# One run over sixteen groups of heads: the next batch prepared one ahead, its parts read back group by group, the splits on GpSimd

## The chip, the core and the metric

The kernel runs on one core of a Trainium2 chip. A core has five engines with an instruction queue each: TensorE (PE, with its weight loads as PEld), VectorE (DVE), ScalarE (ACT), GpSimd (POOL) and SyncE (SP), which here only issues DMAs. All work out of an on-chip memory (SBUF); matmuls write to a second one (PSUM, eight banks of 128 x 512 float32). Engines wait for each other on semaphores. The metric is the device time of one execution in microseconds (us), lower is better.

## What is computed

Four stages run one after the other on x of shape (4, 1024, 128), each between layernorms: a local attention, a mixture of experts, a global causal attention and a six-layer local transformer. The change is in the third, `fourier_attention_stage`. Cut to what matters:

```python
b, t, d = x.shape                                   # 4, 1024, 128; 16 heads of 8
q, k, v = jnp.split(x @ Wqkv.T, 3, axis=-1)         # then heads(...)
logits = jnp.einsum('bhqd,bhkd->bhqk', q, k) * scale
logits = logits + _fourier_bias(alpha, beta, t)[None]   # sum of cos and sin of i - j, per head
logits = jnp.where(causal[None, None], logits, -jnp.inf)
attn = jax.nn.softmax(logits, axis=-1)
out = jnp.einsum('bhqk,bhkd->bhqd', attn, v)
return out.transpose(0, 2, 1, 3).reshape(b, t, d) @ Wout.T
```

## The kernel before

**Parts.** Scores are made by bf16 matmuls whose rows are three-way splits of float32 values: a high part, and two remainders. ACT makes the high part (`parts[:, 0, :]`), and `split` makes the other two, a subtraction and a cast each. A head's rows in `qp` and `kp` (98 partitions x 16 heads x 1024 tokens) are 48 rows of q and k parts, 48 rows of the bias's cosine basis, and two rows for the negated row maximum. As q and k come with features on the partitions, the parts go out to DRAM (`q_dram`, `k_dram`) and come back rearranged, 8 partitions at a time: `d h t` in the code. The k side of the basis (the f parts) takes the same way once, at the start.

**A batch** has a preparation (PE turns x, multiplies by the q, k and v weights; ACT copies out; the splits on DVE; write and read-back by SP), four groups of four heads, and a finish (normalised output turned, times w_out, copied to y_all by DVE).

**A group** has two passes. The maxima pass: PE makes 48 tiles of scores (L737) into two banks, DVE reduces each to its row maxima (L866), then the negated maxima are turned by PE (L781), split in two bf16 rows by DVE (`c_mrow`, L891 to L895) and written over DRAM into `qp` (L687, L689). The second pass: PE makes 40 tiles of transposed scores (L752), ACT takes the exponent (L834), PE multiplies by v (L766). `groups()` overlaps them: the maxima pass of group g + 1 is interleaved with the second pass of group g. In front of a batch stands a maxima pass alone, `body(None, ...)`, and at its end a second pass alone, `body(NG - 1, ..., False)`. PE enters the batch's first maxima pass only when all parts of the batch are placed. Lines here are those of the kernel before.

The order of work on each engine is the order of the code; `Fori` is a loop on the engine itself, and `bass.ds(g, ...)` an address from its register. Every engine runs the same loops, and all of SP's DMAs share one queue.

Of the kernel before, what the change touches and what calls it, by code (L numbers as in the profile page):

```python
# [568 lines left out]
def fourier_attention_stage(nc, y_all, const, dram):  # L569
# [12 lines left out]
    with ExitStack() as ctx:  # L582
# [21 lines left out]
        ve = sb("ve", [P, TB, H, DH + 1])  # L604
# [12 lines left out]
        q_dram = nc.dram_tensor("c_q_scratch", (3, P, SEQ), BF16, kind="Internal").ap()  # L617
        m_dram = nc.dram_tensor("c_m_scratch", (2, GROUP * TB, P), BF16, kind="Internal").ap()
        k_dram = nc.dram_tensor("c_k_scratch", (3, P, SEQ), BF16, kind="Internal").ap()
# [16 lines left out]

        c_in, zeroed, f_done, f_ready, parts_ready, out_dram_done, placed = (
# [11 lines left out]
        def groups(eng, b, body):  # L649

            NG = H // GROUP
            body(None, b * NG - 1, True)
            with eng.Fori(0, NG - 1) as g:
                body(g, b * NG + g, True)
            body(NG - 1, b * NG + NG - 1, False)

        with nc.Block() as block:
            @block.sync
            def _(eng):
                for dst, src in ((ident_b, "ident_b"), (mask_q, "c_mask_q"), (mask_k, "c_mask_k"), (w_qkv, "c_w_qkv"),  # L660
                                 (w_out, "c_w_out"), (place, "c_place"), (basis, "c_basis")):
                    eng.dma_start(dst[:], dram[src]).then_inc(c_in, 16)
# [6 lines left out]
                eng.dma_start(k_dram.rearrange("r p t -> p r t"), kparts[:]).then_inc(out_dram_done, 16)  # L669
                eng.wait_ge(out_dram_done, 16)  # L670
                for r in range(PARTS):
                    eng.dma_start(kp[ROWS + 8 * r:ROWS + 8 * r + 8, :, :],
                                  k_dram[K_PART[r]].rearrange("(h d) t -> d h t", d=DH)).then_inc(placed, 16)
                eng.wait_ge(placed, 16 * PARTS)
                with eng.Fori(0, BATCH) as b:
# [3 lines left out]
                    eng.dma_start(k_dram.rearrange("r p t -> p r t"), kparts[:]).then_inc(out_dram_done, 16)  # L679
# [1163 lines left out]
```

## Time and profile before

| | |
|---|---|
| median of three runs | 6686.75 us (6683.01 to 6694.7) |
| the profiled execution | 6685.4 us, its span 6683.6 us |
| busy in the span | PE 79%, DVE 63%, ACT 44%, POOL 39% |
| the changed stage | 1294.36 to 2956.30 us of the span |
| granted PE clock, mean | 0.895 of full speed |

The span is what the profiler records between the first and last instruction. The stage in question is a quarter of it. The shares of the whole span say little about it; GpSimd, for one, does nothing in it but two memsets.

### The profile page before, as it was taken

The numbers are of one execution on the slowest core, as the hardware profiler recorded it, in microseconds if no ns is written. First come the engines' busy times: TensorE is split into PE (matmuls) and PEld (weight loads), VectorE is DVE, ScalarE is ACT, GpSimd is POOL, SyncE is SP. The second block draws the span as 40 slices with busy tenths as digits, with TensorE's granted clock in tenths as the row PEclk, the third lists the DMA queues.
The fourth block names the chain that finished last, engine by engine and source line by source line (L and its number), as shares of the span: only waits on it lengthen the run. The fifth ranks groups of instructions, "written<-read, shape, count | busy, mean of one in ns | idle before, by whom it ended". The sixth has DMA issues, their size and how long they took to land. (4 is left out here: it accounts for less than half of the span.)

```text
span 6683.6 us, 148998 instructions
## 1 busy us (share of the span) xinstructions
PE 5256.6 (79%) x55030; PEld 3176.6 (48%) x55030; DVE 4233.4 (63%) x5698; ACT 2953.9 (44%) x4797; POOL 2630.1 (39%) x1392
## 2 busy tenths in 40 slices
PE   4735777348488584867999999999999999999996
PEld 3623444212122121214666666666666666666664
DVE  4353111324142332348999989898889888989995
ACT  0001222113123131325666666666666666666663
POOL 0000000000000000017777777677766766777773
PEclk8657889769788686889999999999999999999997
DMA  0000100130200102002111211211121112111111
GB/s 18 0 8 14 28 28 28 20 43 0 29 0 1 28 1 28 1 15 64 36 38 37 57 36 36 57 35 37 34 57 36 35 41 53 36 36 42 35 38 46
DMA packets 153483, 202.80 MB, mean 30 GB/s; under 512 B 40920, under 2 KB 79714, under 8 KB 151662
## 3 DMA queue, kind: packets, MB, share of 16 engines
q1 hardware_dynamic: 153360, 201.17, 13.2%
q8 instruction: 76, 1.25, 0.1%
q14 instruction: 47, 0.39, 0.0%
HBM read 63.67 MB, written 11.53 MB: 11 GB/s over the span
## 5 line engine op out<-in xcount | busy, mean ns | idle before, releaser
L99 POOL TENSOR_TENSOR ln_post_rstd<-ln_post_var,neg_half 128x8 f32<-128x8 f32 x16 | 26.8, 1672 | 2919.6 <-DVE ln_post_var L80 2919.6
L1704 POOL TENSOR_TENSOR d_rnorm<-d_sq_clip,neg_half 128x32 f32<-128x32 f32 x192 | 1048.4, 5461 | 62.6 <-DVE d_sq_clip L1536 61.9
L1694 POOL TENSOR_TENSOR d_qk_swap<-d_qk_raw,d_rot 128x512 f32<-128x512 f32 x768 | 961.0, 1284 | 17.9 <-ACT d_qk_raw L1379 14.0
L866 DVE TENSOR_REDUCE c_mx<-c_ps 128x1 f32<-128x512 f32 (+3 forms) x768 | 416.6, 556 | 775.7 <-PE c_ps L737 771.9
L834 ACT ACTIVATE c_pt<-c_ps 128x512 f32<-128x512 f32 (+1 forms) x640 | 354.3, 554 | 1117.6 <-PE c_ps L752 1115.7
L1153 PE MATMUL d_pair<-d_wqkv,d_xin 128*128 (+1 forms) x1536 | 753.4, 614 | 93.5 <-DVE d_probs L1557 40.6
L766 PE MATMUL c_ps<-c_pt,c_vg 128*32 128x512 f32 (+3 forms) x1536 | 628.3, 506 | 4.7 <-DVE c_ots L871 4.7
L1681 POOL TENSOR_TENSOR d_probs<-d_probs,d_prec 128x1024 f32<-128x1024 f32 x192 | 369.2, 1923 | 454.3 <-DVE d_prec L1568 454.3
L1165 PE MATMUL d_pair<-ident,d_qk_part 128*128 128x128 f32 x3072 | 424.4, 277 | 140.3 <-DVE d_qk_part L1547 137.7
L1165 PEld LDWEIGHTS d_pair<-ident,d_qk_part 128*128 128x128 f32 x3072 | 353.2, 141 | 321.1 <-issue 241.9
L1518 DVE TENSOR_TENSOR d_qk_part<-d_qk_raw,d_rot 128x1024 f32<-128x1024 f32 x384 | 471.4, 1228 | 48.9 <-issue 38.3
L1379 ACT ACTIVATE d_qk_raw<-d_pair 128x512 f32<-128x512 f32 x768 | 424.4, 591 | 94.3 <-PE d_pair L1153 90.3
L1547 DVE TENSOR_TENSOR d_qk_part<-d_qk_part,d_rnorm 128x2048 f32<-128x2048 f32 x192 | 442.2, 2303 | 27.8 <-POOL d_rnorm L1704 4.6
L1543 DVE TENSOR_TENSOR d_qk_part<-d_qk_part,d_qk_swap 128x2048 f32<-128x2048 f32 x192 | 440.0, 2292 | 30.7 <-issue 27.6
L1153 PEld LDWEIGHTS d_pair<-d_wqkv,d_xin 128*128 128x128 f32 x1536 | 280.9, 193 | 349.9 <-issue 332.1
L1532 DVE TENSOR_REDUCE d_sq_sum<-d_qk_sq 128x32 f32<-128x2048 f32 x192 | 433.6, 2258 | 9.7 <-ACT d_qk_sq L1386 6.6
L1173 PE MATMUL d_pair<-d_wqkv,d_xin 128*128 (+1 forms) x768 | 414.4, 621 | 11.3 <-ACT d_kt L1396 9.3
L1402 ACT ACTIVATE d_ot<-d_pair 128x1024 f32<-128x1024 f32 x192 | 196.5, 1023 | 470.7 <-PE d_pair L1209 470.7
L1386 ACT ACTIVATE d_qk_sq<-d_qk_raw 128x1024 f32<-128x1024 f32 x384 | 395.5, 1058 | 6.1
L1205 PE MATMUL d_pair<-d_band,d_v 128*64 128x128 f32 x6144 | 379.8, 276 | 9.3 <-issue 2.0
L1205 PEld LDWEIGHTS d_pair<-d_band,d_v 128*64 128x64 f32 x6144 | 333.5, 137 | 97.2 <-issue 97.0
L557 DVE TENSOR_TENSOR b_part<-b_py,b_b 128x512 f32<-128x512 f32 x64 | 44.2, 691 | 526.1 <-PE b_py L452 526.1
(248 smaller groups left out, 9676.4 us busy)
## 6 DMA issues: line engine op xcount, KB each, us to landing
d_band<-d_own_t SPq DMA_DIRECT2D x768, 64.0 KB, 2.0
d_band<-d_prev_t SPq DMA_DIRECT2D x576, 64.0 KB, 2.0
d_v_prev<-d_v SPq DMA_DIRECT2D x192, 128.0 KB, 2.3
b_w<-in_L_ffn_w SPq DMA_DIRECT2D x64, 256.0 KB, 3.3
d_band_prev<-d_prev_t SPq DMA_DIRECT2D x192, 64.0 KB, 2.0
d_wqkv<-in_L_ffn_Wqkv SPq DMA_DIRECT2D x6, 1536.0 KB, 8.8
c_kp<-c_k_scratch SPq DMA_DIRECT2D x30, 256.0 KB
c_qp<-c_q_scratch SPq DMA_DIRECT2D x24, 256.0 KB
```

The costliest lines, as they stand in the source:

```text
L766: mm = eng.matmul(ps[32 * hh:32 * hh + 32, OB, q0:q0 + nq], vg[:, kt, hh, :], pt[j % 4][:, col:col + nq], start=(opens and k == 0), stop=T ...
L866: eng.tensor_reduce(mx[:, hh, qt, k0 // 512:k0 // 512 + 1], ps[:, S1B[c % 2], 0:nk], AX.X, ALU.max).then_inc(mx_done, 1)
L1153: eng.matmul(bank(QK_AT[u][c]), xin[p][:, :], wqkv[:, bass.ds(par, 1), c * 512:(c + 1) * 512].rearrange("p l n -> p (l n)"), start=True, s ...
L1165: mm = eng.transpose(bank(TURN_AT[u][c])[:, j * P:(j + 1) * P], qk_part[1 - p][:, which, h:h + 2, :].rearrange("p h d -> p (h d)"), ident[ ...
L1205: eng.matmul(op[r:r + 64, h // 2, :].rearrange("p (w t) -> p w t", t=WIN), v_sb[1 - p][:, h * DH:(h + 1) * DH], band[1 - p][:, :, at, :], ...
L1379: eng.activation(qk_raw[:, c // 2, 8 * (c % 2):8 * (c % 2) + 8, :].rearrange("p h d -> p (h d)"), bank(QK_AT[u][c]), ACT.Copy).then_inc(qk ...
L1518: return eng.tensor_tensor(qk_part[p][:, which], qk_raw[:, which], rot[:, bass.ds(par, 1), which, 0, bass.ds(i, 1), :].rearrange("p l t d ...
L1532: eng.tensor_reduce(sq_sum[:], qk_sq[:].rearrange("p a h d -> p (a h) d"), AX.X, ALU.add)
L1543: eng.tensor_tensor(flat, flat, qk_swap[:].rearrange("p a h d -> p (a h d)"), ALU.add)
L1547: eng.tensor_tensor(heads, heads, rnorm[:, :].unsqueeze(2).broadcast_to((P, 2 * HEADS, DH)), ALU.mult).then_inc(rope_ready, 1)
L1694: mm = eng.tensor_tensor(qk_swap[:, which, :, out:out + hd], qk_raw[:, which, :, src:src + hd], rot[:, bass.ds(par, 1), which, 1, bass.ds( ...
L1704: eng.tensor_tensor(rnorm[:, :], sq_clip[:, :], neg_half[:, 0:2 * HEADS], ALU.pow).then_inc(rn_ready, 1)
```

## The change

The four batches become one run. `batches()` takes the place of `groups()`: batch 0 is prepared and the one maxima pass by itself is made; then, for three batches, the next batch is prepared, four groups run, each with the maxima pass of the group behind it (the last one with that of the next batch's first group), and the batch is finished; the last batch's four groups and finish follow. SP reads the next batch's parts back for one group at a time, into the place of the group whose second pass has just ended. v gets two buffers (`ve`), the DRAM copies one place for each batch. The splits go from DVE to GpSimd. The first three constants get a semaphore of their own.

```diff
-        ve = sb("ve", [P, TB, H, DH + 1])
+        ve = sb("ve", [P, 2, TB, H, DH + 1])
...
-        def groups(eng, b, body):
-            NG = H // GROUP
-            body(None, b * NG - 1, True)
+        PLACED = 16 * 2 * PARTS
+        def batches(eng, prepare, body, finish):
+            prepare(0)
+            body(None, 0, -1, True)
+            with eng.Fori(0, BATCH - 1) as b:
+                prepare(b + 1)
+                with eng.Fori(0, NG) as g:
+                    body(g, b, b * NG + g, True)
+                finish(b)
             with eng.Fori(0, NG - 1) as g:
-                body(g, b * NG + g, True)
-            body(NG - 1, b * NG + NG - 1, False)
+                body(g, BATCH - 1, (BATCH - 1) * NG + g, True)
+            body(NG - 1, BATCH - 1, BATCH * NG - 1, False)
+            finish(BATCH - 1)
...
-                for dst, src in ((ident_b, "ident_b"), (mask_q, "c_mask_q"), (mask_k, "c_mask_k"), (w_qkv, "c_w_qkv"),
-                                 (w_out, "c_w_out"), (place, "c_place"), (basis, "c_basis")):
+                for dst, src in ((place, "c_place"), (basis, "c_basis"), (w_qkv, "c_w_qkv")):
+                    eng.dma_start(dst[:], dram[src]).then_inc(first_in, 16)
+                for dst, src in ((ident_b, "ident_b"), (mask_q, "c_mask_q"), (mask_k, "c_mask_k"), (w_out, "c_w_out")):
                     eng.dma_start(dst[:], dram[src]).then_inc(c_in, 16)
...
+                def keep_parts(b):
                     eng.wait_ge(parts_ready, b + 2)
-                    eng.wait_ge(out_done, b)
-                    eng.dma_start(q_dram.rearrange("r p t -> p r t"), qparts[:]).then_inc(out_dram_done, 16)
-                    eng.dma_start(k_dram.rearrange("r p t -> p r t"), kparts[:]).then_inc(out_dram_done, 16)
-                    eng.wait_ge(out_dram_done, b * 32 + 48)
+                    eng.dma_start(one(q_dram, b).rearrange("r p t -> p r t"), qparts[:]).then_inc(out_dram_done, 16)
+                    eng.dma_start(one(k_dram, b).rearrange("r p t -> p r t"), kparts[:]).then_inc(out_dram_done, 16)
+
+                def place_parts(b, g):
+                    eng.wait_ge(placed, (b * NG + g) * PLACED + 16 * PARTS)
                     for r in range(PARTS):
-                        eng.dma_start(qp[8 * r:8 * r + 8, :, :], q_dram[Q_PART[r]].rearrange("(h d) t -> d h t", d=DH)).then_inc(placed, 16)
-                        eng.dma_start(kp[8 * r:8 * r + 8, :, :], k_dram[K_PART[r]].rearrange("(h d) t -> d h t", d=DH)).then_inc(placed, 16)
+                        for to, src, part in ((qp, q_dram, Q_PART[r]), (kp, k_dram, K_PART[r])):
+                            rows = src[bass.ds(b, 1), part, :, :].rearrange("l p t -> (l p) t").rearrange("(h d) t -> d h t", d=DH)
+                            eng.dma_start(to[8 * r:8 * r + 8, bass.ds(g * GROUP, GROUP), :],
+                                          rows[:, bass.ds(g * GROUP, GROUP), :]).then_inc(placed, 16)
+
+                def place_maxima(g, G):
+                    eng.wait_ge(m_ready, G + 1)
+                    ...
+                keep_parts(0)
+                eng.wait_ge(out_dram_done, 48)
+                for g in range(NG // 2):
+                    place_parts(0, g)
+                place_maxima(0, 0)
+                for g in range(NG // 2, NG):
+                    place_parts(0, g)
+                with eng.Fori(0, BATCH - 1) as b:
+                    keep_parts(b + 1)
+                    with eng.Fori(1, NG) as g:
+                        place_maxima(g, b * NG + g)
+                        eng.wait_ge(out_dram_done, b * 32 + 80)
+                        eng.sem_inc(passed, 1)
+                        eng.wait_ge(s2_ready, (b * NG + g) * N2)
+                        eng.sem_inc(passed, 1)
+                        place_parts(b + 1, g - 1)
+                    place_maxima(0, b * NG + NG)
+                    eng.wait_ge(s2_ready, (b * NG + NG) * N2)
+                    eng.sem_inc(passed, 1)
+                    place_parts(b + 1, NG - 1)
+                with eng.Fori(1, NG) as g:
+                    place_maxima(g, (BATCH - 1) * NG + g)
...
             @block.gpsimd
+                def prepare(b):
+                    split(qparts, qf, 2 * b + 2)
+                    split(kparts, kf, 2 * b + 3)
+                    eng.sem_inc(parts_ready, 1)
...
             @block.tensor
-                eng.wait_ge(c_in, 16 * CONSTS)
+                eng.wait_ge(first_in, 48)
...
-                    eng.wait_ge(placed, (b + 1) * (16 * 2 * PARTS) + 16 * PARTS)
+                    if isinstance(b, int):
+                        eng.wait_ge(c_in, 16 * CONSTS)
+                def body(g, b, G, maxima):
+                    live = g is not None
+                    if maxima:
+                        eng.wait_ge(placed, (G + 2) * PLACED + 16 * PARTS)
...
-                                head = (0 if g is None else (g + 1) * GROUP) + hh
+                            head = (0 if g is None else ((g + 1) % NG) * GROUP) + hh
...
             @block.vector
+                def prepare(b):
+                    rows = y_all[:, bass.ds(b * TB, TB), :]
+                    if not isinstance(b, int):
+                        eng.wait_ge(turned, b)
+                    eng.tensor_copy(xin[:], rows).then_inc(xin_ready, 1)
```

The bodies of a group are otherwise the same on all engines, and the diff's other lines only indent them.

PE at the start of a group run, before (the rows behind the first two products; `c_xin` is the batch's x, `ISA` a wait or register load):

```order
L707 UNCONDITIONAL_BRANCH
L707 ISA
L710 MATMUL c_ps<-ident,c_xin 128x128 x8
L715 MATMUL c_ps<-c_xt,c_w_qkv 128x512 x4
L718 MATMUL c_ps<-c_w_qkv,c_xt 128x128 x8
L721 ISA
L723 ISA
L736 MATMUL c_ps<-c_mask_q,c_ident_b 128x128
```

PE in the changed kernel, from the end of the maxima pass that stands alone (the last row of scores and the turn of `c_negm`) to the first tiles of the loop of groups:

```order
L810 MATMUL c_ps<-c_kp,c_qp 128x512
L854 MATMUL c_ps<-ident,c_negm 32x128
L659 UNCONDITIONAL_BRANCH
L659 ISA
L777 MATMUL c_ps<-ident,c_xin 128x128 x8
L782 MATMUL c_ps<-c_xt,c_w_qkv 128x512 x4
L785 ISA
L787 MATMUL c_ps<-c_w_qkv,c_xt 128x128 x8
L790 ISA
L661 UNCONDITIONAL_BRANCH
```

The preparation now stands behind a maxima pass, and what follows it is the loop of groups.

PE in the changed kernel, from the end of the loop of groups to the end of the outer loop:

```order
L854 MATMUL c_ps<-ident,c_negm 32x128
L661 REGISTER_ALU
L661 COMPARE_AND_BRANCH
L857 REGISTER_ALU
L859 MATMUL c_ps<-ident,c_on 128x128 x8
L863 MATMUL c_ps<-c_w_out,c_ont 128x128 x8
L659 REGISTER_ALU
L659 COMPARE_AND_BRANCH
```

Finish (L859, L863) now comes behind a group that carries the next batch's maxima (the turn of `c_negm`).

DVE before, at the head of its loop over batches (the splits of q and k behind the copy of x):

```order
L853 UNCONDITIONAL_BRANCH
L853 ISA
L855 COPY c_xin<-y_all 128x1024
L844 ISA
L846 TENSOR_TENSOR c_qf<-c_qf,c_qparts 128x1024
L848 CAST c_qparts<-c_qf 128x1024
```

DVE in the changed kernel at the same place, the head of its outer loop:

```order
L659 UNCONDITIONAL_BRANCH
L659 ISA
L923 ISA
L923 COPY c_xin<-y_all 128x1024
L661 UNCONDITIONAL_BRANCH
L661 ISA
L931 TENSOR_REDUCE c_mx<-c_ps 128x1
```

Behind the copy of x DVE goes straight to the first row maxima; the subtractions and casts stand on POOL now.

SP in the changed kernel, in the loop over a batch's groups (the maxima's two DMAs, then the first of the twelve of `place_parts`):

```order
L723 ISA
L708 DMA c_m_scratch<-c_mrow 32x2x128
L709 REGISTER_ALU
L710 ISA
L710 DMA c_qp<-c_m_scratch 2x4096
L725 ISA
L727 REGISTER_ALU
L699 ISA
L703 ISA
L703 REGISTER_ALU
L703 DMA c_qp<-c_q_scratch 8x4x1024
```

The read-back of a quarter (8x4x1024 where it was 8x16x1024) now stands behind each group's maxima.

## Rows read from the trace of the kernel before

**Rows 1.** The page's first line.
```profile
span 6683.6 us, 148998 instructions
```

**Rows 2.** Timeline, SP's DMA issues: start us, us, engine, line, what, count.
```profile
1294.36 0.34 SPq L662 DMA_DIRECT2D c_ident_b<-in_ident_b  x1
...
1336.49 0.41 SPq L669 DMA_DIRECT2D c_k_scratch<-c_kparts  x1
1340.10 2.73 SPq L672 DMA_DIRECT2D c_kp<-c_k_scratch  x6
1368.92 0.39 SPq L678 DMA_DIRECT2D c_q_scratch<-c_qparts  x1
...
1374.57 0.31 SPq L682 DMA_DIRECT2D c_qp<-c_q_scratch  x1
...
1379.12 4.55 SPq L682 DMA_DIRECT2D c_qp<-c_q_scratch  x1
```

**Rows 3.** Stretches: from:to, length, busy by engine (x instructions), PEclk, DMA share, GB/s.
```profile
1766.00:1834.00 68.00, 0.55 (x4) 0.35 (x4) 4.32 (x6) 0.47 (x1) 0.00 (x0) 0.52 0.50 70
...
2013.00:2087.00 74.00, 65.94 (x265) 20.32 (x265) 29.94 (x59) 22.64 (x41) 0.00 (x0) 0.89 0.00 0
...
1374.60:1432.50 57.90, 0.00 (x0) 0.00 (x0) 0.00 (x0) 0.00 (x0) 0.00 (x0) 0.50 0.52 54
```

**Rows 4.** Waits of 1294 to 2957 us: total us, times, longest us.
```profile
PE c_ps L736 <- DMA c_kp<-c_k_scratch: 291.3, 4, 84.3
```

**Rows 5.** Timeline, PE's first products and the first maxima pass [idle before <- releaser].
```profile
1326.36 3.78 PE L704 MATMUL c_ps<-c_basis,c_place 12*128 12x512 f32 x4 [81.11 <-DMA c_kp<-in_c_ones]
...
1432.51 0.29 PE L736 MATMUL c_ps<-c_mask_q,c_ident_b 128*128 128x128 bf16 x1 [84.28 <-DMA c_kp<-c_k_scratch]
```

**Rows 6.** Timeline, DVE's last c_mrow copy of a maxima pass.
```profile
1466.08 0.21 DVE L895 CAST c_mrow<-c_mrest 32x128 bf16<-32x128 f32 x1
...
1685.86 0.21 DVE L895 CAST c_mrow<-c_mrest 32x128 bf16<-32x128 f32 x1
...
1867.03 0.21 DVE L895 CAST c_mrow<-c_mrest 32x128 bf16<-32x128 f32 x1
...
2088.53 0.21 DVE L895 CAST c_mrow<-c_mrest 32x128 bf16<-32x128 f32 x1
...
2891.90 0.21 DVE L895 CAST c_mrow<-c_mrest 32x128 bf16<-32x128 f32 x1
```

**Rows 7.** Timeline, ends of groups and batches, and one preparation.
```profile
2087.30 0.39 PE L781 MATMUL c_ps<-ident,c_negm 128*32 128x128 f32 x1 [1.41 <-DVE c_negm L886]
...
2092.14 0.29 PE L750 MATMUL c_ps<-c_mask_k,c_ident_b 128*128 128x128 bf16 x1 [4.45 <-DMA c_qp<-c_m_scratch]
...
2145.69 0.26 DVE L876 RECIPROCAL c_rec<-c_ps 128x16 f32<-128x16 f32 x1 [0.84 <-PE c_ps L775]
...
2150.69 1.23 DVE L899 TENSOR_SCALAR y_all<-c_ps 128x1024 f32 x1 [4.38 <-PE c_ps L790]
2155.12 0.69 DVE L855 COPY c_xin<-y_all 128x1024 f32 x1 [3.20 <-issue]
...
2167.33 1.06 ACT L819 ACTIVATE c_ve<-c_ps 128x512 f32<-128x512 f32 x2
...
2545.39 0.26 DVE L876 RECIPROCAL c_rec<-c_ps 128x16 f32<-128x16 f32 x1 [0.84 <-PE c_ps L775]
...
2552.69 1.23 DVE L899 TENSOR_SCALAR y_all<-c_ps 128x1024 f32 x1 [6.68 <-PE c_ps L790]
...
2955.07 1.23 DVE L899 TENSOR_SCALAR y_all<-c_ps 128x1024 f32 x1 [4.38 <-PE c_ps L790]
```

**Rows 8.** Lines and sources: durations ns (mean; or min/median/max) of DVE and POOL operations.
```profile
L846 DVE TENSOR_TENSOR c_kf<-c_kf,c_kparts 128x1024 f32<-128x1024 f32 x10 | 12.3, 1225 | 41.2 <-ACT c_kparts L803 38.8 <-issue 2.1
...
L1681 POOL TENSOR_TENSOR d_probs<-d_probs,d_prec x192: 1894/1903/1987, 3059.1 to 6586.4; 128x1024 f32<-128x1024 f32 x192
L1704 POOL TENSOR_TENSOR d_rnorm<-d_sq_clip,neg_half 128x32 f32<-128x32 f32 x192 | 1048.4, 5461 | 62.6 <-DVE d_sq_clip L1536 61.9
...
L1547 DVE TENSOR_TENSOR d_qk_part<-d_qk_part,d_rnorm x192: 2291/2292/3390, 3033.3 to 6569.2; 128x2048 f32<-128x2048 f32 x192
```

More of the change, by code:

```diff
@@ L672, in _, with one @@
                     eng.dma_start(kp[ROWS + 8 * r:ROWS + 8 * r + 8, :, :],
-                                  k_dram[K_PART[r]].rearrange("(h d) t -> d h t", d=DH)).then_inc(placed, 16)
+                                  f_dram[K_PART[r]].rearrange("(h d) t -> d h t", d=DH)).then_inc(placed, 16)
                 eng.wait_ge(placed, 16 * PARTS)
-                with eng.Fori(0, BATCH) as b:
+                def one(x, b):
+                    return x[bass.ds(b, 1)].rearrange("l r p t -> (l r) p t")
@@ L784, in _, with finish @@
+                def finish(b):
                     eng.wait_ge(on_ready, (b + 1) * 8)
@@ L793, in _ @@
                     eng.wait_ge(batch_done, b + 1)
+                batches(eng, prepare, body, finish)
             def flat(x):
@@ L836, in _, with body @@
-                    groups(eng, b, body)
+                def body(g, b, G, maxima):
+                    if g is not None:
+                        eng.wait_ge(pv_done, G * N2)
+                        eng.activation(vg[:, :, :, 0:DH + 1].rearrange("p t h d -> p t h d"),
+                                       ve[:, bass.ds(b % 2, 1), :, bass.ds(g * GROUP, GROUP), :].rearrange("p l t h d -> p (l t) h d"), ACT.Copy).then_inc(vg_ready, 1)
+                        for c in range(N2):
+                            width = sum(s[2] for s in S2[c][2])
+                            eng.wait_ge(s2_ready, G * N2 + c + 1)
+                            if c >= 4:
+                                eng.wait_ge(pv_done, G * N2 + c - 3)
+                            eng.activation(pt[c % 4][:, 0:width], ps[:, S2B[c % 4], 0:width], ACT.Exp).then_inc(exp_done, 1)
@@ L837, in _, with finish, prepare @@
+                def finish(b):
                     eng.wait_ge(on_turned, b + 1)
                     eng.activation(ont[:, :], flat(ps[:, 0:2, :]), ACT.Copy).then_inc(ont_ready, 1)
+                batches(eng, prepare, body, finish)
             @block.vector
             def _(eng):
-                def split(parts, full, count):
-                    eng.wait_ge(hi_ready, count)
-                    for k in (1, 2):
-                        eng.tensor_tensor(full[:, :], full[:, :], parts[:, k - 1, :], ALU.subtract)
+                def prepare(b):
+                    rows = y_all[:, bass.ds(b * TB, TB), :]
+                    if not isinstance(b, int):
+                        eng.wait_ge(turned, b)
+                    eng.tensor_copy(xin[:], rows).then_inc(xin_ready, 1)
@@ L900, in _ @@
                     eng.drain().then_inc(batch_done, 1)
+                batches(eng, prepare, body, finish)
 def local_transformer_stage(nc, y_store, x_store, const, dram, x_parked):
```

237 lines of the change are left out of this document (115 added, 122 removed).

## The prediction

> **What bounds the kernel now.** I read the page first (how long the profiled execution is [rows 1]), then the busy time by stretches, then the waits of the stage that the diff touches, and last the timeline around one hand-over between batches. The stage runs from the first constant's DMA at 1294.36 [rows 2] to the end of the last output copy, 2955.07 + 1.23 = 2956.30 [rows 7]: 1661.9 us of the span. Everything after it waits for it, so what it gives up comes off the end.
>
> In a batch there are two kinds of stretch. In the group stretches PE is busy 65.94 of 74 us [rows 3]; a group's period, from one c_mrow copy to the next, is (1685.86 - 1466.08) / 3 = 73.3 us in batch 0 and (2088.53 - 1867.03) / 3 = 73.8 us in batch 1 [rows 6]: 73.5. Between batches nothing computes: from 1766 to 1834 PE is busy 0.55 us while half of the DMA capacity (share 0.50) reads the parts back [rows 3]. The waits put 291.3 us in four waits on this read-back [rows 4]. It comes before the maxima of a batch's first group, which run by themselves: 1432.51 to 1466.08, 33.6 us [rows 5, 6]. The last group of a batch runs by itself too: from its c_mrow copy to the end of finish it is 2150.69 + 1.23 - 2088.53 = 63.4 us in batch 1 and 2955.07 + 1.23 - 2891.90 = 64.4 in the last [rows 6, 7]; 64.
>
> **The change, as a new timeline.** I add up the new stage from its start; its end against 2956.30 is the gain. T0 is the start of the last c_mrow copy of a maxima pass.
>
> First read-back. PE starts its two cosine products once three constants are there, no longer when the last has landed (it waited to 1326.36 [rows 5]). The gain is not those 30 us: the f parts, ready about 1315 (a few us for the DMAs, 3.8 for the products, about 2 on ACT, a split on GpSimd), are written on the same queue behind six constants of 256 KB, which still land near 1326. The write took 3.6 us [rows 2]; between "landed together with them" (1326.4) and "wholly behind them" (1330.0) I take the middle, 1328. Then come the six reads of f, 1368.92 - 1340.10 = 28.8 us [rows 2], to 1356.8, the two writes of batch 0, 1374.57 - 1368.92 = 5.7 us, to 1362.5, and one group's read-back. The twelve old DMAs of 256 KB took 1432.51 - 1374.57 = 57.9 us [rows 2, 5]; the new ones carry a quarter each in the same 2 KB rows over the same eight partitions, and the old ones moved at a steady share of 0.52 [rows 3]. So 57.9 / 4 = 14.5, and 1.5 for start and landing: PE begins its first maxima at 1378.5, not at 1432.5. Upper bound: if each DMA costs the same whatever its size, 57.9 again. Twelve DMAs of a quarter should not fill the queue: the long issues (4.55 us) start with the ninth full-size one [rows 2], when eight times 128 rows of 2 KB are out; twelve times 32 are 384.
>
> First maxima 33.6 us: T0 = 1412.1.
>
> Preparation of batch 1, now after this pass. c_xin at 2155.12 to the end of the c_ve copies at 2167.33 + 1.06 is 13.3 us, 0.4 of loop and wait behind it [rows 7]: 13.7. c_xin starts right behind the pass on DVE, so the scores of group 0 start at T0 + 14 instead of T0 + 3.6 (2092.14 - 2088.53 [rows 6, 7]), the wait for the c_mrow DMAs being hidden under it: 10.4 us more.
>
> Groups: 15 of the 16 now carry the maxima of the next one, across batches too: 15 x 73.5 = 1102.5 us. Bounds 73.3 and 73.8: 1099 and 1107.
>
> Two hand-overs with finish and preparation (batches 0 to 1 and 1 to 2). PE's turn of c_negm starts 1.2 us ahead of T0 and takes 0.39 [rows 6, 7], and finish's transposes follow at T0 - 0.8. From the last reciprocal to the end of the output copy it is 6.2 us in one batch (2145.69 to 2151.92) and 8.5 in another (2545.39 to 2553.92), where PE ran slower [rows 7]; 0.7 of it lies ahead of the transposes. A group that carries maxima ends in waits on DVE, so I take the slower: output copy ends at T0 - 0.8 + 7.8 = T0 + 7.0. Then 3.2 us of loop [rows 7], then 13.7: T0 + 23.9 instead of T0 + 3.6, 20.3 us each; with the faster finish 18. I take 20: 40 us. The third hand-over (2 to 3) has finish alone: T0 + 7.1 at most, 3.5 more, 1.2 at least; 3.
>
> Last group and finish: 64 us.
>
> Sum: 1412.1 + 10.4 + 1102.5 + 40 + 3 + 64 = 2632.0. Gain 2956.3 - 2632.0 = **324 us**. The profiled execution took 6685.4 (span 6683.6 [rows 1]); the median of the runs is 1.4 higher. 6686.8 - 324 = 6362.8; the twelve periods of all batches come out a shade under my 73.5 in the two batches not shown, so I say **6361**.
>
> **Edits costed at nothing.** The splits on GpSimd: DVE needed 1225 ns for a subtraction and GpSimd 1903 for a two-input operation of the same 128x1024 [rows 8]. The cast is not shown there; between nothing and the 5461 of GpSimd's power function I take 1.5 us, nearer to the plain operation. A batch's eight are about 14 us, at worst 8 x 5.5 = 44. They start 10 to 20 us behind T0 and are wanted when SP comes to keep_parts, ahead of the next group's maxima, 84 to 94 behind it. Even 44 is covered. Only in front are they near the path: the K split of batch 0 starts at about 1332 after Q's at 1330, both done by 1344 to 1374, wanted at 1356.8: 0, at worst 17 us. If the cover were gone, SP would reach place_maxima late, and PE's first score of the next group, and ACT's exponents behind it, would stand for the excess.
>
> The Trainium skill speaks against this step: its GPSIMD Engine Reference (3.1, elementwise) measures a two-input addition at 1.96 times DVE's time and keeps elementwise work on DVE. The trace agrees in kind: 1903 against 1225 is 1.55 times. By the page's ratio a split's subtractions are 2 x 2.4 us; the sum stays the same either way, since what counts is the cover.
>
> The per-group read-back: 12 issues right behind the c_qp maxima DMA in SP's order, 12 to 20 us of DMA under a group of 73.5. PE asks at the top of group G for the parts of group G + 1, while SP has issued those of G + 2 and issues G + 3, so it is over a period early. The bigger c_ve memset is about 1 us on an idle GpSimd.
>
> **Rivals.** (a) The groups get longer: GpSimd's splits or the DMAs now run beside them. DVE instructions beside a busy GpSimd were stretched from 2292 to at most 3390 ns [rows 8]; 1.1 us x 8 operations x 3 batches is 26 us if PE had no slack, and a us more in each group from the DMAs is 15 more: 6361 + 41 = 6402. Against it: DVE is busy 29.94 of 74 us there [rows 3], and its reductions read PSUM. The Trainium skill (SBUF — State Buffer, who interferes with whom) says that the two engines share a port pair that one locks for a whole instruction, but that tensor_reduce never contends on this chip; by that it is zero, and no row of this stage can show it, since GpSimd is idle in it. (b) The DMA cost is per DMA, not per byte: 57.9 us for each group. The first one is 42 us later; groups 2 and 3 of batch 0 are then issued behind the first maxima, one after the other, and the maxima of group 1 come some 40 us late: 6361 + 85 = 6446. (c) The change doesn't do what it says: PE still waits for a read-back at each batch. Then three times the write and read-back of 57.9 + 5.7 us comes back: 6361 + 191 = 6552. The counts of placed speak against it. (d) It ends slower. SP takes every DMA in one queue, and place_maxima of the next group stands behind the twelve issues of place_parts. If an issue with register addresses costs so much that SP needs longer than 73.5 us for a group, all later groups wait for it. It eats the 324 us over 12 groups at 27 us each, that is, 100 us or 8.4 us an issue. Rows 2 have 0.31 and 4.55 us. At 9 us an issue: 6361 + 12 x (108 - 73.5) = 6775. (e) Better: with no long idle stretches PE's clock (0.52 in the idle stretch, 0.89 in the group's [rows 3]) stays up through hand-overs: 5 us there and a us in each group, 6341.
>
> **How the numbers follow.** Chances: my sum 0.70, (a) 0.11, (b) 0.04, (c) 0.02, (d) 0.03, (e) 0.10. The range reaches from (e) to just short of (a)'s far end: 6338 to 6396; the prologue's worst 17 + 2 us and the hand-overs' bounds fall inside. A measurement of this kernel tells 0.2% (13 us). Faster by more holds in all cases but (d): 0.96; the same 0.01; slower 0.03.
>
> **What would show it.** PE's wait for the read-back gone but for one of some 50 us in front; first maxima near 1378; c_mrow copies 73 to 74 us apart within a batch and about 93 over two of the hand-overs; 15 waits for c_m_scratch less three; GpSimd's casts; and the stage's end near 2632. The prediction fails if the groups of a batch's first 20 us stretch, if SP's issues with registers take microseconds, or if falling out of the inner loop costs PE what the outer loop costs DVE (3.2 us [rows 7], at most 3 x 3.2).

## The result, and the profile after

| | before | after |
|---|---|---|
| median | 6684.88 us (6681.73 to 6694.7, 4 runs) | 6363.49 us (6356.39 to 6367.86, 4 runs) |
| ratio, with 95% interval | | 0.9518 (0.9504 to 0.9532) |
| the profiled execution, its span | 6685.4, 6683.6 us | 6366.8, 6365.1 us |
| the stage, first constant's DMA to last output copy | 1661.9 us | 1328.0 us |
| granted PE clock, mean | 0.895 | 0.914 |

The forecast was 6361 with a range of 6338 to 6396. The page of the changed kernel begins (its first line, and part 1, the busy time by engine):

```profile
span 6365.1 us, 149552 instructions
...
PE 5238.0 (82%) x55030; PEld 3186.2 (50%) x55030; DVE 4208.1 (66%) x5662; ACT 2952.3 (46%) x4796; POOL 2688.6 (42%) x1428
```

The waits of the stage in the changed kernel (us in total, times, longest):

```profile
POOL c_qf L750 <- ACT c_qparts L892: 687.4, 4, 296.8
...
PE c_ps L809 <- DMA c_kp<-c_k_scratch: 64.3, 3, 60.3
...
PE c_ps L823 <- DMA c_qp<-c_m_scratch: 46.4, 12, 4.6
```

The four waits for the read-back [rows 4] have become one of 60.3 us in front. The other two, 2.0 us each, are put down to the read-back but end otherwise: at 1424.66 and 2343.01 the parts that PE asks for had been placed long before, and at the second it starts 0.6 us behind DVE's output copy. The waits for the maxima are twelve, some 3.9 us each: four of the sixteen maxima passes (the one in front and the three at a change of batch) have a preparation or a finish behind them that hides the wait, the other twelve, the last one among them, have not.

The timeline of the front in the changed kernel (start us, us, engine, line, what; idle time and its end in brackets); it answers to [rows 2] and [rows 5]:

```profile
1297.30 0.38 SPq L673 DMA_DIRECT2D c_place<-in_c_place  x1
...
1300.50 3.78 PE L770 MATMUL c_ps<-c_basis,c_place 12*128 12x512 f32 x4 [52.34 <-DMA c_w_qkv<-in_c_w_qkv]
...
1313.36 0.40 SPq L682 DMA_DIRECT2D c_f_scratch<-c_kparts  x1
...
1332.03 2.41 SPq L685 DMA_DIRECT2D c_kp<-c_f_scratch  x6
1334.36 2.12 POOL L750 TENSOR_TENSOR c_qf<-c_qf,c_qparts 128x1024 f32<-128x1024 f32 x1 [21.07 <-ACT c_qparts L892]
1336.61 1.04 POOL L752 CAST c_qparts<-c_qf 128x1024 bf16<-128x1024 f32 x1
...
1357.39 0.40 SPq L694 DMA_DIRECT2D c_q_scratch<-c_qparts  x1
...
1363.06 0.31 SPq L703 DMA_DIRECT2D c_qp<-c_q_scratch  x1
...
1376.95 0.26 PE L809 MATMUL c_ps<-c_mask_q,c_ident_b 128*128 128x128 bf16 x1 [60.26 <-DMA c_kp<-c_k_scratch]
```

PE starts 3.2 us behind the first constant's issue, and the f parts are written at 1313.36. But SP goes on only at 1332.03, when that write has landed behind the other constants. From there it is reads of f, writes of batch 0, one group's read-back, and the first maxima at 1376.95.

The timeline of one hand-over, batch 0 to batch 1, in the changed kernel (the last `c_mrow` copy of the group ahead, then finish and preparation), which answers to [rows 7]:

```profile
1713.97 0.21 DVE L960 CAST c_mrow<-c_mrest 32x128 bf16<-32x128 f32 x1
...
1720.07 1.23 DVE L965 TENSOR_SCALAR y_all<-c_ps 128x1024 f32 x1 [5.88 <-PE c_ps L863]
1721.99 0.69 DVE L923 COPY c_xin<-y_all 128x1024 f32 x1 [0.69 <-issue]
...
1731.25 2.14 POOL L750 TENSOR_TENSOR c_qf<-c_qf,c_qparts 128x1024 f32<-128x1024 f32 x1 [296.76 <-ACT c_qparts L892]
1733.52 1.04 POOL L752 CAST c_qparts<-c_qf 128x1024 bf16<-128x1024 f32 x1
...
1735.21 0.22 PE L809 MATMUL c_ps<-c_mask_q,c_ident_b 128*128 128x128 bf16 x1 [2.02 <-ACTq L897]
```

PE is on the next scores 21.2 us behind the `c_mrow` copy. From the end of the output copy to the next scores it is 1735.21 - 1721.30 = 13.9 us; at the same place the kernel before took 1833.45 - 1749.20 = 84.3. The gap between the output copy and the copy of the next x is 0.69 us; it was 3.17 there and 3.20 in [rows 7].

Stretches of the changed kernel (columns as in [rows 3]): the first group's read-back, the first group with GpSimd's splits beside it, the second without them:

```profile
1363.00:1376.90 13.90, 0.00 (x0) 0.00 (x0) 0.00 (x0) 0.00 (x0) 0.00 (x0) 0.50 0.44 57
1424.00:1494.50 70.50, 65.16 (x267) 19.92 (x267) 29.79 (x59) 22.97 (x43) 9.58 (x7) 0.93 0.15 35
1494.50:1567.00 72.50, 63.70 (x265) 19.59 (x265) 29.65 (x59) 22.64 (x41) 0.00 (x0) 0.92 0.08 11
```

The groups look as they did. From `c_mrow` copy to `c_mrow` copy, the twelve plain groups of the kernel before (those with neither a preparation nor a finish) took 73.33 us on average and the eleven of the changed one 73.22. In both kernels they come in two kinds, about 72.7 us at a mean granted clock of 0.92 and about 74.1 at 0.89; seven were of the first kind in either. Across a change of batch the clock is no longer low. Before, batch 0 to 1, and after:

```profile
1685.86:1867.03 181.17, 90.06 (x323) 30.29 (x323) 37.81 (x69) 30.99 (x50) 0.00 (x0) 0.68 0.19 27
```

```profile
1713.97:1804.99 91.02, 79.32 (x320) 29.24 (x319) 31.95 (x61) 31.38 (x51) 12.65 (x8) 0.88 0.11 26
```

The stage ends at 2624.06 + 1.23 = 2625.29:

```profile
2559.54 0.21 DVE L960 CAST c_mrow<-c_mrest 32x128 bf16<-32x128 f32 x1
...
2624.06 1.23 DVE L965 TENSOR_SCALAR y_all<-c_ps 128x1024 f32<-128x1024 f32 x1 [6.68 <-PE c_ps L863]
```

**The stage against the whole.** The stage gave up 1661.9 - 1328.0 = 333.9 us, the profiled execution 6685.4 - 6366.8 = 318.6. The other 15.3 us are outside the changed code. The stage started 2.9 us later (1297.30 against 1294.36). The stretch behind it, from the fourth stage's first constant to the end of the span, took 3693.8 us where it had taken 3681.2, with the same code. In the experiments below I therefore read the length of the stage from the trace, and the medians beside it.

### The profile page after: what moved, and what is told of

The parts are those of the page before. It is cut to its first block and busy times, and to the rows that moved or that the text cites. A ratio compares the mean times of both kernels' runs of the same rounds, so it can differ in the third digit from the quotient of the medians.

```text
span 6365.1 us, 149552 instructions
## 1 busy us (share of the span) xinstructions
PE 5238.0 (82%) x55030; PEld 3186.2 (50%) x55030; DVE 4208.1 (66%) x5662; ACT 2952.3 (46%) x4796; POOL 2688.6 (42%) x1428
## 5 line engine op out<-in xcount | busy, mean ns | idle before, releaser
L1762 POOL TENSOR_TENSOR d_qk_swap<-d_qk_raw,d_rot 128x512 f32<-128x512 f32 x768 | 960.1, 1283 | 16.5 <-ACT d_qk_raw L1447 15.3
L1586 DVE TENSOR_TENSOR d_qk_part<-d_qk_raw,d_rot 128x1024 f32<-128x1024 f32 x384 | 471.8, 1229 | 47.6 <-issue 34.2
L1241 PE MATMUL d_pair<-d_wqkv,d_xin 128*128 (+1 forms) x768 | 417.6, 626 | 11.9 <-ACT d_kt L1464 10.8
```

What stands on the lines that cost most here:

```text
L1586: return eng.tensor_tensor(qk_part[p][:, which], qk_raw[:, which], rot[:, bass.ds(par, 1), which, 0, bass.ds(i, 1), :].rearrange("p l t d ...
L1762: mm = eng.tensor_tensor(qk_swap[:, which, :, out:out + hd], qk_raw[:, which, :, src:src + hd], rot[:, bass.ds(par, 1), which, 1, bass.ds( ...
```

## The experiments

There are eight edits, and copies of the two kernels. Each ratio is against the kernel before as timed beside that run: its median was 6684.88 us beside the changed kernel, 6694.48 beside e1, e2, e3 and e6, and 6680.26 beside e4, e5, e7 and e8. Medians of different groups are therefore compared by their ratios.

| kernel | median us | ratio (95%) | stage us | against after |
|---|---|---|---|---|
| after | 6363.49 | 0.9518 (0.9504 to 0.9532) | 1328.0 | |
| e1, splits back on DVE | 6382.34 | 0.9532 (0.9519 to 0.9545) | 1344.8 | +16.8 |
| e2, before + read-back by group | 6515.03 | 0.9733 (0.9718 to 0.9748) | 1494.9 | +166.9 |
| e3, before + splits on GpSimd | 6698.13 | 1.0007 (0.9998 to 1.0016) | 1667.7 | +339.7 |
| e4, GpSimd's work some 55 us | 6356.31 | 0.9519 (0.9505 to 0.9534) | 1329.5 | +1.5 |
| e5, GpSimd's work some 97 us | 6472.72 | 0.9693 (0.9678 to 0.9707) | 1447.0 | +119.0 |
| e6, PE waits for all constants | 6393.18 | 0.9547 (0.9534 to 0.9560) | 1344.8 | +16.8 |
| e7, groups written out | 6366.34 | 0.9533 (0.9517 to 0.9549) | 1340.0 | +12.0 |
| e8, six score tiles ahead | 6310.18 | 0.9451 (0.9438 to 0.9463) | 1279.1 | -48.9 |

### One part alone, or undone

**e1_dve_splits**: the changed kernel with `split` and its calls moved from GpSimd back to DVE.

```diff
             @block.vector
+                split(kparts, kf, 1)
+                eng.sem_inc(parts_ready, 1)
                 def prepare(b):
                     ...
                     eng.tensor_copy(xin[:], rows).then_inc(xin_ready, 1)
+                    split(qparts, qf, 2 * b + 2)
+                    split(kparts, kf, 2 * b + 3)
+                    eng.sem_inc(parts_ready, 1)
```

> The changed kernel with its splits back on DVE, all else as changed. Mine: the splits are off the path on GpSimd; on DVE they stand ahead of the first row maxima of each batch's first group, and in the kernel before they ended 5 us behind the c_ve copies. So about 5 us at each of three preparations, first group of a batch 5 us longer: 15 us slower than the changed kernel, 6378. Rival (GpSimd's work beside the groups costs them something): same or faster, 6363 or less.

Measured: stage +16.8 us. From `c_mrow` copy to `c_mrow` copy the three groups with a preparation took 88.42, 95.75 and 94.92 us instead of 83.97, 91.02 and 91.02: 13.1 us together. Some 4.4 us are lost at each preparation, where the splits stand on DVE between the copy of x and the next row maxima. The other 3.7 us lie where the edit does nothing (1.3 in front, 1.7 in one more plain group of the slower kind, 1.0 at the last change of batch), so the splits account for 13 to 17 us.

**e2_groupwise_only**: the kernel before, its batches still apart, but each batch read back group by group, twelve DMAs of four heads a group.

```diff
+                    def place_parts(g):
+                        eng.wait_ge(placed, (b * 4 + g) * PLACED + 16 * PARTS)
                         ...
+                    place_parts(0)
+                    place_parts(1)
+                    place_maxima(0)
+                    place_parts(2)
+                    place_parts(3)
...
-                    eng.wait_ge(placed, (b + 1) * (16 * 2 * PARTS) + 16 * PARTS)
+                        if maxima:
+                            eng.wait_ge(placed, (G + 2) * PLACED + 16 * PARTS)
```

> The kernel before with one part of the change: the read-back group by group (groups 0 and 1, the maxima of group 0, groups 2 and 3), PE waiting for the group it needs. Mine: the read-back's time goes by bytes, so a batch's first maxima start after 14 us and not after 58: 4 x 43 = 172 us faster than before, 6513. Rival (a DMA costs the same whatever its size): no gain, and a loss behind the first group.

Measured: stage 1661.9 - 1494.9 = 167.0 us shorter. Its wait for the read-back in the waits of the stage:

```profile
PE c_ps L749 <- DMA c_kp<-c_k_scratch: 118.6, 4, 39.8
```

The wait fell by 291.3 - 118.6 = 172.7 us in four batches, 43.2 each, against three quarters of 57.9 = 43.4. So DMAs of a quarter cost a quarter, and half of the stage's gain needs no run over batches at all. The gap from the output copy to the copy of x stayed as before, 3.28 us.

**e3_pool_splits_only**: the kernel before with the splits on GpSimd.

```diff
             @block.vector
-                split(kparts, kf, 1)
-                eng.sem_inc(parts_ready, 1)
                 with eng.Fori(0, BATCH) as b:
                     eng.tensor_copy(xin[:], rows).then_inc(xin_ready, 1)
-                    split(qparts, qf, 2 * b + 2)
-                    split(kparts, kf, 2 * b + 3)
-                    eng.sem_inc(parts_ready, 1)
```

and the same calls on GpSimd.

> The kernel before with one part of the change: the splits on GpSimd. There they are on the path of batches 1 to 3. Mine: four operations take 13.7 us by the trace of the changed kernel, against 8.7 from the high part of q to DVE's last cast: 5 us in three batches, batch 0 hidden behind the read of the f parts, 16 us slower than before, 6701. Rival (as fast as on DVE where nothing runs beside it): 6685.

Measured: stage +5.8 us against the kernel before (+9.2 against its copy r2), and a ratio that doesn't differ from 1. The sign was as expected, the size a third to a little over half of it. The trace between batches 0 and 1:

```profile
1753.91 1.23 DVE L901 TENSOR_SCALAR y_all<-c_ps 128x1024 f32 x1 [4.38 <-PE c_ps L806]
1755.80 0.69 DVE L860 COPY c_xin<-y_all 128x1024 f32 x1 [0.67 <-issue]
...
1779.02 0.39 SPq L678 DMA_DIRECT2D c_q_scratch<-c_qparts  x1
```

The same place in the kernel before:

```profile
1747.98 1.22 DVE L899 TENSOR_SCALAR y_all<-c_ps 128x1024 f32 x1 [4.38 <-PE c_ps L790]
1752.37 0.69 DVE L855 COPY c_xin<-y_all 128x1024 f32 x1 [3.17 <-issue]
...
1771.01 0.39 SPq L678 DMA_DIRECT2D c_q_scratch<-c_qparts  x1
```

The write of q came 1779.02 - 1755.14 = 23.9 us behind the output copy, before 1771.01 - 1749.20 = 21.8. From the copy of x to the write it is 23.2 us against 18.6: 4.6 slower on GpSimd. But the copy of x itself came 2.5 us sooner, because DVE's gap at the end of its loop fell from 3.17 to 0.67 us with the splits' instructions gone from the loop's body. I had missed that half.

**e6_all_constants**: the changed kernel, where PE waits for every constant after all.

```diff
                 eng.wait_ge(first_in, 48)
+                eng.sem_inc(passed, 1)
+                eng.wait_ge(c_in, 16 * CONSTS)
```

> The changed kernel, but PE waits for all constants before its cosine products, as before. Mine: the f parts come some 29 us later but their write then finds an empty queue and takes 3.6 us in place of 18.7: first maxima about 14 us later, 6377. Rival (the early start buys nothing, since the queue decides): 6363. Rival (it buys all of the 29 us): 6392.

Measured: stage +16.8 us, of which 15.5 lie ahead of the first maxima pass's end (128.7 us from the stage's start instead of 113.2). In its timeline:

```profile
1329.95 3.78 PE L772 MATMUL c_ps<-c_basis,c_place 12*128 12x512 f32 x4 [80.31 <-DMA c_kp<-in_c_ones]
...
1342.81 0.40 SPq L682 DMA_DIRECT2D c_f_scratch<-c_kparts  x1
1346.42 2.31 SPq L685 DMA_DIRECT2D c_kp<-c_f_scratch  x6
...
1374.27 0.40 SPq L694 DMA_DIRECT2D c_q_scratch<-c_qparts  x1
```

With nothing ahead of it in the queue the write lands in 3.6 us; in the changed kernel it took 1332.03 - 1313.36 = 18.7. PE began 1329.95 - 1298.78 = 31.2 us behind the stage's start in e6 and 1300.50 - 1297.30 = 3.2 in the changed kernel. Of these 28 us only 15.5 arrive, because the write waits behind the constants. And 2.5 of the 15.5 are not the edit's: the six reads of f took 1374.27 - 1346.42 = 27.9 us in e6 and 25.4 in the changed kernel, a term that moves by itself (see below). Up to the landing of f it is 47.6 us from the stage's start against 34.7, or 12.9 us. The median is 11 us above that of e1, whose stage is as long; the last stretch of e6's profile was the longest of all, 3704.4 us.

### How much cover GpSimd has

**e4_pool_55us** and **e5_pool_97us**: the changed kernel with each cast of batches 1 to 3 made 11 times and 21 times (the second has 20 where the diff has 10); the output stays the same.

```diff
-                        eng.tensor_copy(parts[:, k, :], full[:, :])
-                        eng.drain()
+                        for _ in range(1 + extra):
+                            eng.tensor_copy(parts[:, k, :], full[:, :])
+                            eng.drain()
...
-                    prepare(b)
+                    prepare(b, 10)
```

> The changed kernel, GpSimd doing each cast of batches 1 to 3 eleven times over: 40 more casts, 60 us a batch in place of 14. Mine: covered, since the next group's maxima are due 84 to 91 us behind T0 and it ends at 70 to 77; no change, 6363. Rival (GpSimd beside the groups stretches them): some us in each batch's first group, up to 40 x 1.1 = 44 us a batch, 6363 to 6495.

> The same with each cast 21 times over: 80 more casts, about 106 us a batch. Mine: the cover is gone. SP comes to keep_parts some 32 us too late for the maxima of the second group, and their DMAs stand behind a write of 5 us: 37 us in each of three batches, 6474, and it shows as PE's wait for the c_m_scratch DMA in the second group. Rival (SP's wait for the parts holds nobody): 6363.

Measured in e4: nothing (stage +1.5 us; the copies below differ by 0.9), with GpSimd busy 51.46 us of the first 69 of a group and the write of q at 1478.13 - 1292.76 = 185.4 us from the stage's start, where the changed kernel had it at 1434.72 - 1297.30 = 137.4. Two stretches of e4:

```profile
1420.00:1489.00 69.00, 62.58 (x266) 19.25 (x266) 29.35 (x58) 23.80 (x44) 51.46 (x47) 0.97 0.16 36
1489.00:1563.00 74.00, 65.78 (x266) 20.23 (x265) 29.97 (x59) 22.64 (x41) 0.00 (x0) 0.89 0.09 11
```

DVE does the same work in the same time beside a GpSimd that is busy three quarters of the stretch. The durations of its row maxima (min/median/max in ns), in the changed kernel:

```profile
L931 DVE TENSOR_REDUCE c_mx<-c_ps x768: 281/620/693, 1377.4 to 2554.1; 128x1 f32<-128x512 f32 x128, 128x1 f32<-128x128 f32 x64
```

and in e4:

```profile
L932 DVE TENSOR_REDUCE c_mx<-c_ps x768: 281/620/693, 1373.6 to 2552.6; 128x1 f32<-128x512 f32 x128, 128x1 f32<-128x128 f32 x64
```

They are the same. The Trainium skill says in SBUF — State Buffer (who interferes with whom) that tensor_reduce never contends with GpSimd on this chip, and the trace agrees. These reductions read PSUM, so the durations say nothing of one that reads SBUF.

In e5 the cover is gone, and the second group of each batch is longer. It shows where it was expected, as PE's wait for the maxima (41.8, 43.0 and 43.0 us in these groups):

```profile
PE c_ps L824 <- DMA c_qp<-c_m_scratch: 162.5, 12, 43.0
```

SP's DMA issues around the first of them:

```profile
1529.07 0.42 SPq L694 DMA_DIRECT2D c_q_scratch<-c_qparts  x1
1529.59 0.43 SPq L695 DMA_DIRECT2D c_k_scratch<-c_kparts  x1
1530.29 0.84 SPq L708 DMA_DIRECT2D c_m_scratch<-c_mrow  x1
1535.13 0.27 SPq L710 DMA_DIRECT2D c_qp<-c_m_scratch  x1
```

The maxima of that group were ready at 1495.5 and left at 1530.29, because SP stood in `keep_parts` in front of them. Second groups took 112.34, 111.86 and 111.92 us instead of 72.78, 72.75 and 72.72: 117.9 of the 119.0 us. Queue order decides: the late parts were not wanted before the batch's last group, the maxima behind them at once.

### The loop's end

**e7_unrolled**: the changed kernel with the four groups of the three batches written out instead of looped.

```diff
-                with eng.Fori(0, NG) as g:
+                for g in range(NG):
                     body(g, b, b * NG + g, True)
```

> The changed kernel with the inner loop over four groups written out four times, so that the outer loop's code is some 3.5 times as long. Between the output copy and the c_xin copy DVE stood 3.2 us in the kernel before and 0.7 in the changed one. Mine: that gap goes by the length of the code that the jump goes back over; it is 3.2 us again at two hand-overs, 5 us in all, 6368. Rival (the gap hangs on something else, such as the splits behind c_xin): 0.7 us, 6363.

Measured: stage +12.0 us, more than twice what I had said. DVE at the hand-over from batch 0 to 1:

```profile
1714.54 1.22 DVE L965 TENSOR_SCALAR y_all<-c_ps 128x1024 f32 x1 [5.72 <-PE c_ps L863]
1724.46 0.69 DVE L923 COPY c_xin<-y_all 128x1024 f32 x1 [8.70 <-issue]
```

The hand-overs took 98.61 and 97.50 us, not 91.02: 14.1 us, of which 3.0 came back in a shorter first group (80.94 against 83.97, but 82.46 and 83.28 in the copies of the changed kernel, so part of it is scatter). DVE's gap from output copy to x copy, by the instructions that its code has once between the outer loop's head and its end (drains not counted, some to the next five): after 125, 0.69 us; e1 135, 0.70; e3 236, 0.67; before and e2 246, 3.2 and 3.3; e7 457, 8.70 and 8.83. That the rival fails is shown by e1: there the splits stand behind the copy of x again, and the gap is 0.70. So whether there is a long gap goes by the body's length, in e3 against before and in e7 against the changed kernel.

The profile also has the queue by which code comes in. Its DMA packets (queue, kind: packets, MB, share of the DMA engines) for the kernel before, from the end of the output copy at 1749.20 to the copy of x at 1752.37:

```profile
q14 instruction: 1, 0.01, 0.9%
```

Each of the three gaps of that kernel has one such packet, and so has the gap in e2. From 1730 to 2900 the kernel before has 15 of them, five in each batch, of 8 KB each; e3 has none in that stretch, and the changed kernel none from 1550 to 2350. So with the longer bodies code is fetched again in every pass, and with the shorter ones it is not. In e7, from 1715.76 to 1724.46:

```profile
q1 hardware_dynamic: 295, 0.48, 43.7%
q8 instruction: 1, 0.02, 1.1%
q14 instruction: 1, 0.01, 0.5%
```

Here too there is one, but the read-back of a group runs at the same time on the same DMA engines (q1, SP's queue), where the kernel before had nothing else in its gap. So the step from 3.2 to 8.7 us is not shown to come of the length alone; the read-back in the fetch's way is a rival that no run parts from it. That DVE stands because it waits for its code fits the times and the counts; the profile doesn't say which engine's code a packet carries.

### A better version

**e8_lead6**: in the changed kernel PE waits some 3.9 us behind each maxima pass for the maxima to come through DRAM, while the next group's first score tiles wait for nothing. Six of them go ahead, on PE and on DVE.

```diff
+        LAG, LEAD = 2, 6
...
+                    lead = LEAD if maxima and live else 0
+                    for c in range(lead):
+                        scores(c)
+                    for c in range(max(N1 - lead if maxima else 0, N2 + LAG if live else 0)):
+                        if maxima and c + lead < N1:
+                            scores(c + lead)
```

`scores` is the old loop's piece for one tile; DVE has `reduced` in the same order.

> The changed kernel with one change of order, on PE and DVE alike: in a group that carries maxima, the first six of its 48 score tiles come ahead of the loop, under the wait for the c_m_scratch and c_qp DMAs of the maxima, and none is left over behind the loop. Mine: that wait of 3.9 us in 12 groups goes, the six tiles (4 us, set by DVE) take its place, and 3 us of tail go: 3 us in each of 15 groups, 6318. Rival (the tiles cost as much in front as behind): 6363.

Measured: 6310.18 us, stage 48.9 us shorter than the changed kernel's, a little more than I had expected. Plain groups took 68.7 to 70.2 us, 69.4 on average, instead of 73.2. The timeline behind one `c_mrow` copy of e8:

```profile
1491.81 0.22 PE L807 MATMUL c_ps<-c_mask_q,c_ident_b 128*128 128x128 bf16 x1 [0.40 <-issue]
...
1492.25 0.21 DVE L971 CAST c_mrow<-c_mrest 32x128 bf16<-32x128 f32 x1
...
1492.49 0.34 SPq L708 DMA_DIRECT2D c_m_scratch<-c_mrow  x1
...
1496.47 0.31 PE L828 MATMUL c_ps<-c_mask_k,c_ident_b 128*128 128x128 bf16 x1
```

PE works from 1491.81 and takes up the second pass at 1496.47, 4.2 us behind the `c_mrow` copy, with no wait for the maxima. In the changed kernel it stood from there to 1498.48, 4.0 us behind the copy at 1494.48, and its scores came after. Eleven plain groups at 3.84 us less are 42.2 of the 48.9; the rest is spread over the other groups in ones and twos. The waits for the maxima fell from 46.4 us in twelve to 4.5 in one, that of the last group, which has no score tiles to put ahead. So the gain is the wait itself, in eleven groups, and not 3 us in each of fifteen as I had put it. Other counts than six were not run.

### The same kernels again

**r1_changed_again**, **r3_changed_third** and **r2_before_again** are copies, to see what moves by itself.

> The changed kernel once more, for its profile. In the ten profiles so far the stretch from the fourth stage's first constant DMA to the end is 3676.8 to 3704.4 us, with the same code for that stage; the changed kernel had 3693.8 and the one before 3681.2. Mine: that stretch differs from execution to execution, so it moves by some us here, while the attention stage is 1328 +- 2 us again. Rival (the change lengthens the fourth stage by 12.6 us): 3694 again.

> The kernel before once more, for its profile. Mine: attention stage 1662 +- 4 us, the fourth stage's stretch anywhere in 3677 to 3704. Rival (it goes by the kernel): 3681 again.

> The changed kernel a third time. Mine: attention stage 1328 +- 2, the last stretch elsewhere than in the other two profiles of the same kernel by some us. Rival: 3694 again.

| profiled execution | stage us | last stretch us | stage begins at |
|---|---|---|---|
| after, r1, r3 | 1328.0, 1328.1, 1328.9 | 3693.8, 3694.1, 3699.4 | 1297.3, 1298.8, 1296.8 |
| before, r2 | 1661.9, 1658.5 | 3681.2, 3687.5 | 1294.4, 1294.6 |
| e1 to e8 | as above | 3680.0, 3676.8, 3688.6, 3687.6, 3682.9, 3704.4, 3684.4, 3680.0 | 1292.8 to 1298.8 |

The stage repeats within 1 us in the changed kernel and 3.4 in the one before. The last stretch of r1, 3694.1, is what the rival said, and not what I had said; r2 and r3 speak against the rival by some 6 us each. The stretch behind the stage moves by about 6 us between executions of one kernel and by 28 over all kernels. In the changed kernel it lay some 11 us above the one before on average, and its stage began 2 to 4 us later; whether that belongs to the kernel (where its code and buffers lie) or to chance, three profiles against two don't settle. The six edits of the changed kernel (e1, e4 to e8) speak against its being the change: their last stretch is 3686.6 us on average, within 3 us of the kernel before's 3684.4. It stays open, and it is some 15 us of a gain of 320.

## Why the prediction was right

**The sum, term by term**, in us; "measured" is from the changed kernel's profile. T0 is the start of the last `c_mrow` copy of a maxima pass.

| term | predicted | measured |
|---|---|---|
| start to the landing of f | 33.6 | 1332.03 - 1297.30 = 34.7 |
| six reads of f | 28.8 | 1357.39 - 1332.03 = 25.4 |
| two writes | 5.7 | 1363.06 - 1357.39 = 5.7 |
| one group's read-back | 16.0 | 1376.95 - 1363.06 = 13.9 |
| first maxima pass | 33.6 | 1410.51 - 1376.95 = 33.6 |
| first preparation | 10.4 | 83.97 - 73.2 = 10.8 |
| 15 groups | 1102.5 | 15 x 73.22 = 1098.3 |
| two hand-overs | 40 | 2 x (91.02 - 73.22) = 35.6 |
| third hand-over | 3 | 77.58 - 73.22 = 4.4 |
| last group and finish | 64 | 2625.29 - 2559.54 = 65.8 |
| stage | 1337.6 | 1328.0 (rounding apart) |

The stage was 9.6 us shorter than forecast: 4.5 in front, 4.2 in the groups, 4.4 in the hand-overs, less 3.5 in the other terms. The 15.3 us outside the stage took back more than that: the profiled execution came to 6366.8, and the median is 3.3 below it, at 6363.5 against 6361. So errors cancelled, and that the forecast of the whole is so close is in part luck. Without the 15.3 us the median would have been 6348, still inside the range.

**In front.** The write of f was taken at the middle between landing with the constants and wholly behind them. It was wholly behind: in e6 the constants are there 1329.95 - 1298.78 = 31.2 us from the start, and 31.2 + 3.6 = 34.8. By e6 the early start is worth 12.9 us up to there, of PE's 28. The read-back of a group at 57.9 / 4 was right within 2 us, and e2 shows the quarter again in four batches. The reads of f were 3.4 us shorter than before; over all profiles they took 25.4 to 28.9 us (26.1 in r2, the copy of the kernel before, and 28.6 in e5), so this term is loose by some 3 us; why is not shown. PE's wait in front was 60.3 us and not some 50, since PE was through with its own work sooner, at 1316.7; the first maxima came at 1376.95, as forecast.

**Groups.** Neither GpSimd's splits nor the DMAs made them longer (rival (a)): 73.22 us on average over eleven plain groups, and e4, with four times the work on GpSimd, shows room beyond that. Rival (e) had its condition, a clock that stays up across a change of batch (0.88 for 0.68), but not its price: the groups run at 0.92 or 0.89 as before, and a plain group is 0.1 us shorter, 73.22 for 73.33. My 73.5 was the mean of two batches that held three of the slower kind in six; the twelve together have five.

**Hand-overs.** One term was off, the 3.2 us of loop at DVE's end: it measured 0.69. I had carried the gap over from the loop before, though the splits that left DVE and the new nesting made the loop's body half as long. Twice 2.5 us are 5.0; the forecast was 4.4 too high, since the rest of the hand-over was right within 0.6 us (output copy ends at T0 + 7.3, predicted 7.0). e3, and the packets of code, tie the gap to the length of the body.

**The splits.** Costed at nothing, by their cover. GpSimd's subtraction took 2.12 us (I had costed it by the 1.9 of [rows 8]) and the cast 1.04 (I had taken 1.5), so a batch's eight took 1346.90 + 1.04 - 1334.36 = 13.6 us, as in the estimate of 14. e1 shows that the move is more than harmless: 13 to 17 us of the gain. The forecast had this implicitly, by leaving DVE's splits out of the preparation. e3 shows that the same edit alone is worth nothing or a little less, since there the parts are waited for. The Trainium skill's GPSIMD Engine Reference (3.1, elementwise) gives GpSimd 1.96 times DVE's time for a two-input float32 addition and keeps elementwise work on DVE. Here it was 2122 against 1225 ns, 1.73 times, with one input bf16. On the path the rule holds (e3: 4.6 us more from the copy of x to the write of q), off it moving the work paid (e1).

**The other rivals.** (b), a cost for each DMA whatever its size: 13.9 us for the first group where it wanted 57.9, and e2. (c): the waits are gone. (d), a queue that falls behind: issues with register addresses take 0.29 to 0.31 us and stand about 0.5 apart; twelve need 6 us of SP's 73. Its mechanism is real, though. e5 makes SP late by holding it in `keep_parts`, and the excess comes through in full.

**Where the 334 us of the stage came from**, by the experiments: 167.0 by the read-back in groups alone (e2); some 15.5 by the constants (e6); 16.8 by the splits' move, once the run is in place (e1). The other 134.6 remain for the run over all batches with its preparation one ahead. It was not run alone, but e1 and e2 differ by it and the constants only, and their traces say where it lies. In e2 the three stretches over a change of batch took 138.2, 138.2 and 141.3 us from `c_mrow` copy to `c_mrow` copy, in e1 95.8, 94.9 and 78.6, with 88.4 instead of 72.8 in the first group, where batch 1 is prepared: 132.8 us less in all.

## What to carry to other kernels

Before you move work to a slower engine, ask when its result is wanted, not how long it takes: the same splits cost a little with the reader waiting and gained 13 to 17 us with over 40 us of cover. Look at what stands behind the late thing in its queue, since that is what pays (e5). And where an interleaved group begins with a wait for a small round trip through memory, put a few of the next group's tiles ahead of it; six tiles here were worth 49 us, a seventh of what the whole restructuring brought.

## What the hardware showed that I had not expected

- DVE's gap at an outer loop's jump back depends on how much code the body holds: 0.67 to 0.70 us up to 236 instructions, 3.2 us at 246 (drains not counted). The profile shows a packet of code in each long gap, and none in the passes of the shorter bodies. With the inner loop written out (457) it was 8.7 us, with a read-back on the DMA engines at the same time.
- A small write (the f parts) behind large constants on the same queue took 18.7 us (16.7 to 20.3 over the eight profiles of this order) instead of 3.6: its issue was early, its landing was not.
- Stages that nobody touched differ by up to 28 us of 3690 between profiles of different kernels, so that medians hide steps of 10 us which the length of the changed stage shows plainly.
